# Attention and quantized feed-forward on one core: the up bias scaled as one row, and every queue in a new order

## What is computed

```
q = rope(RMS(LN(x)) * q_w)   k = rope(RMS(ctx) * k_w)   v = ctx        (16 query heads, 4 k/v heads of 32)
x = x + softmax(causal(q k^T / sqrt(32))) v  @ w_out^T
h = relu(LN(x) @ w_up + b_up + LN(x) @ A_up @ B_up)                    (2048 columns)
x = x + h @ w_down + b_down + h @ A_down @ B_down
```

## Time and profile before

| | |
|---|---|
| median of the runs | 482.93 us |
| profiled execution, its own time | 484.46 us |
| its span, first to last instruction | 482.7 us |
| mean granted TensorE clock | 0.979 |
| PE busy | 443.0 us (92%), 2416 matmuls |
| DVE busy | 352.0 us (73%) |
| ACT busy | 300.3 us (62%) |
| POOL (GpSimd) busy | 282.1 us (58%) |

### The profile page before, as it was taken

How to read it: one execution, slowest core, us unless ns; L and a number is a source line. 1 busy time by engine, 2 the same in 40 slices (tenths; PEclk the granted TensorE clock), 3 DMA queues, 4 the chain that set the end, 5 groups by cost and what they waited for, 6 DMA issues and landing times.

```text
span 482.7 us, 8285 instructions
## 1 busy us (share of the span) xinstructions
PE 443.0 (92%) x2416; PEld 218.2 (45%) x2416; DVE 352.0 (73%) x1076; ACT 300.3 (62%) x927; POOL 282.1 (58%) x304
## 2 busy tenths in 40 slices
PE   0285869999999999999999999999999999999997
PEld 0164545444444444444444444444444445444443
DVE  3899998979879786868686877778777856534341
ACT  1698978878858675757575757666675856422120
POOL 5477767685859574848384747576657745451100
PEclk9996879999999999999999999999999999999999
DMA  8679769789777858887867777897697777474422
GB/s 224 215 245 175 189 206 209 114 167 141 160 121 137 168 109 160 135 171 114 171 130 155 134 158 132 169 132 161 122 135 163 118 153 110 91 125 93 88 56 74
DMA packets 207740, 70.36 MB, mean 146 GB/s; under 512 B 196880, under 2 KB 200096, under 8 KB 207056
## 3 DMA queue, kind: packets, MB, share of 16 engines
q1 hardware_dynamic: 206864, 69.35, 72.7%
q10 hardware_dynamic: 752, 0.34, 0.3%
q0 software_dynamic: 80, 0.16, 0.2%
HBM read 17.15 MB, written 4.19 MB: 44 GB/s over the span
## 4 chain that ended last, share of the span: by engine, by line
PE 78%; DVE 1%; DMA 1%; SPq 0%; issue 0%
PE ff L951 33%; PE ff L937 33%; PE tb L919 8%; PE sb L891 2%; PE tb L907 2%; DMA x<-hid 1%; SPq L401 0%; PE tb L877 0%; DVE t_sin L1171 0%; DVE pr L1203 0%; DVE y L1253 0%; DVE stats L1184 0%; DVE x L1181 0%; DVE q L1212 0%; DVE q L1118 0%
## 5 line engine op out<-in xcount | busy, mean ns | idle before, releaser
L951 PE MATMUL ff<-wd_hi,x 128*128 128x512 f16 x512 | 152.3, 379 | 0.7 <-DMA x<-hid 0.7
L937 PE MATMUL ff<-wu_hi,xnT 128*128 128x512 f16 x512 | 152.7, 380 | 0.0
L691 ACT ACTIVATE pr<-pr,nmax 128x128 f32<-128x128 f32 x256 | 99.0, 389 | 13.6 <-DVE nmax L1203 12.9
L515 POOL TENSOR_TENSOR big<-pr,big 128x512 f16<-128x512 f32 x64 | 80.9, 1272 | 32.6 <-ACT big L722 32.6
L937 PE MATMUL ff<-wu_lo,xnT 128*128 128x512 f16 x256 | 97.0, 379 | 0.0
L951 PE MATMUL ff<-wd_lo,x 128*128 128x512 f16 x256 | 97.0, 379 | 0.0
L506 POOL TENSOR_TENSOR pr<-pr,rinv 128x512 f32<-128x512 f32 x64 | 72.7, 1137 | 35.6 <-DVE rinv L1111 35.6
L756 ACT ACTIVATE hid<-z 128x512 f16<-128x512 f32 x64 | 39.9, 624 | 80.1 <-DVE z L1132 80.1
L1203 DVE CUSTOM_DVE_ANT_0 pr<-sb,tabs,score_scale 128x128 f32<-128x128 f32 x256 | 73.8, 344 | 12.3 <-PE sb L891 11.2
L937 PEld LDWEIGHTS ff<-wu_hi,xnT 128*128 128x128 f16 x512 | 48.2, 98 | 58.4 <-issue 5.9
L1132 DVE SCALAR_TENSOR_TENSOR z<-ff,su,b_row 128x512 f32<-128x512 f32 x64 | 47.7, 745 | 36.0 <-PE ff L937 34.7
(11 more groups left out here) (144 smaller groups left out, 652.7 us busy)
## 6 DMA issues: line engine op xcount, KB each, us to landing
xt<-in_x SPq DMA_DIRECT2D x16, 256.0 KB, 3.0
big<-in_L_ffn_w_up_q SPq DMA_DIRECT2D x4, 1024.0 KB, 7.3
big<-in_L_ffn_w_down_q SPq DMA_DIRECT2D x4, 1024.0 KB, 6.2
out<-y SPq DMA_DIRECT2D x16, 256.0 KB, 2.7
wd_lo<-in_L_xattn_w_out SPq DMA_DIRECT2D x1, 1024.0 KB, 7.5
pT<-big SPq DMA_TRANSPOSE x64, 3.5
b_row<-in_L_ffn_b_up SPq DMA_DIRECT2D x1, 1024.0 KB, 9.1
x<-hid SPq DMA_TRANSPOSE x64, 3.2
```

The costliest lines, as they stand in the source:

```text
L515: pool.tensor_tensor(p3[:, m, :, 1, :], pr[:, m], p3[:, m, :, 0, :], ALU.subtract).then_inc(p_low, 1)
L691: last = act.activation(pr[:, m, g, :], pr[:, m, g, :], ACT.Exp, bias=nmax[:, p, j:j + 1], scale=-1.0, accum_out=rsum[:, p, j:j + 1])
L937: last = pe.matmul(bank[:], a[:, m, :], b[:, m, 512 * g:512 * g + 512], start=(m == 0 and i == 0), stop=(m == KC - 1 and i == 2))
L951: last = pe.matmul(ff[down_bank[n]][:], x2T[:, part, k + h % HG, :], b[:, h, :], start=(h == 0 and i == 0), stop=(h == HC - 1 and i == 2))
```

## The change

On the bias: DVE multiplies the 16x128 form of the row by the factor right after the factor is known (`b_scaled`, which lies in the tile z); SP stores these 8 KB to a row in memory (`bias_scaled_row`), and the load of `b_row` reads that row in place of b_up. ACT's four multiplications are gone. The store waits for DVE, the load for the store, and the load of weight group 2, which overwrites `b_flat`, now waits for DVE's multiplication too. z of batch 0 waits once, for the load.

On the order: nearly all slots change, PERIOD and FREE stay. The tiles that DVE dequantizes and those whose low part it makes are chosen anew (27 as before, and 26 for 25); the new slots were planned with longer transfer times. In SP's queue the first entries are now: load of w_out, batch 1, the three moves of LoRA rows, the LoRA factor, weight groups 1 and 2, transposes of q and k of batch 0, the bias store, weight group 3, the bias row. The diff, with the order's constants that the text speaks of:

```diff
@@ -24,84 +24,84 @@
-R_STATS = (0, 19, 407, 1366)
-R_MOMENTS = (2, 33, 483, 1400)
-R_SINES = (12, 110, 554, 1489)
-R_KLOW = (32, 211, 1015, 1496)
-R_QLOW = (18, 345, 975, 1516)
-R_QTURN = (409, 637, 1281, 1619)
-R_PTURN = ((687, 1308, 1751, 1921), (734, 1395, 1767, 2005), (1050, 1432, 1782, 2066), (1056, 1489, 1798, 2080))
-R_VLOW = (639, 1508, 2209, 2641)
-R_OLOW = (657, 1410, 1795, 2120)
-R_XNLOW = (934, 1660, 1960, 2268)
-R_XNTURN = (1268, 1739, 2015, 2244)
-R_UP = ((1254, 1861, 2175, 2525), (1381, 1898, 2244, 2538), (1526, 1935, 2251, 2553), (1632, 1993, 2290, 2592))
-R_Z = ((1159, 1746, 2046, 2325), (1202, 1776, 2109, 2385), (1302, 1864, 2172, 2440), (1467, 1896, 2216, 2495))
-R_X2LOW = ((1194, 1772, 2068, 2345), (1324, 1834, 2190, 2414), (1347, 1918, 2201, 2491), (1518, 1927, 2221, 2509))
-R_DOWN = ((1762, 2065, 2356, 2640), (1778, 2085, 2391, 2656), (1828, 2128, 2441, 2658), (1838, 2134, 2443, 2714))
-R_X2TURN = ((1555, 1867, 2159, 2401), (1563, 1894, 2179, 2428), (1599, 1914, 2205, 2467), (1620, 2002, 2216, 2468))
-DVE_TILES = (0, 1, 2, 3, 4, 5, 6, 7, 8, 9, 10, 12, 13, 14, 15, 16, 17, 18, 19, 20, 22, 23, 24, 25, 27, 28, 30)
-LOW_BY_DVE = (0, 1, 2, 5, 9, 10, 11, 14, 15, 16, 17, 18, 19, 20, 21, 22, 23, 24, 25, 26, 27, 28, 29, 30, 31)
-DEQ_AT = (17, 21, 22, 46, 60, 85, 87, 88, 99, 250, 281, 140, 288, 299, 466, 482, 560, 642, 653, 757, 837, 809, 941, 950, 1012,
-          1061, 1072, 1107, 1197, 1675, 1349, 1831)
-LOAD_AT = (379, 431, 567, 584, 1102, 1178, 1287)
-WO_LOAD_AT = 252
-ROW_LOAD_AT, DOWN_BIAS_LOAD_AT = 1243, 827
-BATCH_LOAD_AT = (116, 550, 1508)
-LORA_B_ROWS_AT = (381, 744)
-LORA_D_LOAD_AT, NORM_SCALES_AT = 115, 1
-BIAS_ROW_AT = (1091, 1190, 1384, 1460)
...
+R_STATS = (0, 52, 481, 1332)
+R_MOMENTS = (5, 179, 596, 1400)
+R_SINES = (35, 232, 818, 1547)
+R_KLOW = (68, 367, 1036, 1551)
+R_QLOW = (97, 484, 1125, 1593)
+R_QTURN = (230, 578, 1243, 1976)
+R_PTURN = ((734, 1503, 2000, 2418), (756, 1580, 2070, 2463), (972, 1597, 2150, 2472), (1062, 1673, 2167, 2491))
+R_VLOW = (981, 1711, 2708, 3025)
+R_OLOW = (1101, 1475, 1955, 2268)
+R_XNLOW = (1273, 1771, 2082, 2352)
+R_XNTURN = (1337, 2085, 2450, 2710)
+R_UP = ((1901, 2249, 2565, 2822), (1922, 2301, 2603, 2862), (2004, 2359, 2639, 2925), (2035, 2393, 2687, 2963))
+R_Z = ((1438, 1873, 2145, 2407), (1444, 1896, 2225, 2497), (1582, 2023, 2245, 2548), (1702, 2024, 2302, 2570))
+R_X2LOW = ((1548, 1929, 2219, 2480), (1581, 1943, 2269, 2537), (1681, 2028, 2301, 2561), (1716, 2056, 2317, 2574))
+R_DOWN = ((2131, 2439, 2712, 2973), (2140, 2447, 2724, 2988), (2212, 2463, 2751, 3037), (2216, 2490, 2792, 3065))
+R_X2TURN = ((1809, 2251, 2540, 2791), (1970, 2262, 2582, 2854), (1982, 2296, 2655, 2924), (2046, 2297, 2692, 2947))
+DVE_TILES = (0, 1, 2, 3, 4, 5, 6, 7, 8, 9, 11, 12, 13, 15, 16, 17, 18, 19, 21, 22, 24, 25, 27, 28, 29, 30, 31)
+LOW_BY_DVE = (2, 4, 6, 8, 9, 10, 11, 12, 14, 15, 16, 17, 18, 19, 20, 21, 22, 23, 24, 25, 26, 27, 28, 29, 30, 31)
+DEQ_AT = (7, 19, 20, 33, 109, 113, 165, 167, 204, 216, 281, 268, 339, 364, 349, 490, 568, 594, 619, 719, 909, 821, 984, 1036,
+          989, 1171, 1545, 1229, 1361, 1374, 1388, 1415)
+LOAD_AT = (174, 202, 334, 542, 726, 896, 1280)
+WO_LOAD_AT = 2
+ROW_LOAD_AT, DOWN_BIAS_LOAD_AT = 376, 1134
+BATCH_LOAD_AT = (97, 434, 1189)
+LORA_B_ROWS_AT = (115, 384)
+LORA_D_LOAD_AT, NORM_SCALES_AT = 125, 2
+BIAS_STORE_AT = 330
...
@@ -166,6 +166,9 @@
 
         s_up_flat, a_dn_flat = big[:, 4096:4096 + HC * C // QB], big[:, 4224:4224 + HC * R]
         b_flat = big[0:HC, 4480:4480 + P]
+
+        b_scaled = z[0:HC, 0, 0:P]
+        b_store = nc.dram_tensor("bias_scaled_row", (H,), F32).ap()
         R3 = 3 * R
 
         b_up_parts = high_area[:, 0:384].bitcast(F16).rearrange("p (k c) -> p k c", k=3)
@@ -247,7 +250,7 @@
         scale_steps, scales_ready = sem("scale_steps"), sem("scales_ready")
         tables_ready, pool_consts = sem("tables_ready"), sem("pool_consts")
         norm_scale_steps = sem("norm_scale_steps")
-        bias_row_in, bias_scaled = sem("bias_row_in"), sem("bias_scaled")
+        bias_row_in, bias_scaled, bias_stored = sem("bias_row_in"), sem("bias_scaled"), sem("bias_stored")
         a_high, a_low, b_high, b_low = sem("a_high"), sem("a_low"), sem("b_high"), sem("b_low")
         ident_cast, minus_cast = sem("ident_cast"), sem("minus_cast")
         a_turned, a_copied = sem("a_turned"), sem("a_copied")
@@ -360,6 +363,7 @@
                     sp.wait_ge(w_turned, 4 * (g - W_RING + 1))
                 if g == 2:
                     sp.wait_ge(tops_ready, 7)
+                    sp.wait_ge(bias_scaled, 1)
                 src = wuq_v[g] if g < 4 else wdq_v[g - 4]
                 sp.dma_start(stage_i[:, g % W_RING], src).then_inc(wq_in[g % W_RING], 16)
 
@@ -433,8 +437,12 @@
                     sp.dma_start(a_nat[:, KC * R:].rearrange("p (g a) -> p g a", a=4 * R), wda_v).then_inc(a_dn_in, 16)
                 if s == WO_LOAD_AT:
                     sp.dma_start(wo_raw, wo.rearrange("(j p) c -> p j c", p=P)).then_inc(wout_in, 16)
+                if s == BIAS_STORE_AT:
+                    sp.wait_ge(bias_scaled, 1)
+                    sp.dma_start(b_store.rearrange("(p a) -> p a", p=HC), b_scaled).then_inc(bias_stored, 16)
                 if s == ROW_LOAD_AT:
-                    sp.dma_start(b_row[:], bu.rearrange("(a n) -> a n", a=1).broadcast_to([P, H])).then_inc(bias_row_in, 16)
+                    sp.wait_ge(bias_stored, 16)
+                    sp.dma_start(b_row[:], b_store.rearrange("(a n) -> a n", a=1).broadcast_to([P, H])).then_inc(bias_row_in, 16)
                 if s == DOWN_BIAS_LOAD_AT:
                     sp.dma_start(bd_bc[:], bd.rearrange("(a n) -> a n", a=1).broadcast_to([P, C])).then_inc(down_bias_in, 16)
                 n = at(s, R_STORE)
@@ -606,12 +614,6 @@
                     act.wait_ge(wout_in, 16)
                 act.activation(wo_nat[:, j, :].rearrange("p (n g d) -> p n g d", g=NG, d=HD),
                                wo_raw[:, j, :].rearrange("p (g n d) -> p n g d", g=NG, d=HD), ACT.Copy).then_inc(wo_ordered, 1)
-
-            def bias_row(g):
-                act.wait_ge(scale_steps, SCALE_STEPS)
-                act.wait_ge(bias_row_in, 16)
-                part = b_row[:, 512 * g:512 * g + 512]
-                act.activation(part, part, ACT.Identity, scale=kap[:, 5:6]).then_inc(bias_scaled, 1)
 
             def lora_a_high(down):
                 if down:
@@ -781,8 +783,6 @@
                         weights_low(t)
                 attention(s)
                 for m in range(4):
-                    if BIAS_ROW_AT[m] == s:
-                        bias_row(m)
                     if WO_ORDER_AT[m] == s:
                         wout_order(m)
                     if WO_HIGH_AT[m] == s:
@@ -1055,6 +1055,7 @@
                 dve.tensor_scalar(s_up[:, 0:4, :], s_up[:, 0:4, :], kap[:, 0:1], None, ALU.mult).then_inc(scales_ready, 1)
                 dve.tensor_scalar(s_dn[:], s_dn[:], kap[:, 1:2], None, ALU.mult).then_inc(scales_ready, 1)
                 link(dve.tensor_scalar(kap[:, 5:6], kap[:, 4:5], X2_TOP, None, ALU.mult))
+                dve.tensor_scalar(b_scaled, b_flat, kap[0:HC, 5:6], None, ALU.mult).then_inc(bias_scaled, 1)
                 link(dve.tensor_scalar(su[:], power[:, 0:1], kap[:, 5:6], -1.0 / XN_SCALE, ALU.mult, ALU.mult), wait=False)
                 link(dve.tensor_scalar(sd[:], power[:, 1:2], power[:, 4:5], 1.0 / X2_TOP, ALU.mult, ALU.mult), wait=False)
                 assert step[0] == SCALE_STEPS
@@ -1127,8 +1128,8 @@
                         dve.wait_ge(up_done, 4 * n + g + 1)
                         if 4 * n + g >= 2:
                             dve.wait_ge(x2_low, 4 * n + g - 1)
-                        if n == 0:
-                            dve.wait_ge(bias_scaled, g + 1)
+                        if n == 0 and g == 0:
+                            dve.wait_ge(bias_row_in, 16)
                         dve.scalar_tensor_tensor(z[:, g % 2], ff[up_bank[n, g]][:], su[:], b_row[:, 512 * g:512 * g + 512],
                                                  ALU.mult, ALU.add).then_inc(ff_read, 1)
```

94 lines of the change are left out of this document (47 added, 47 removed).

## The result

The changed kernel took **490.66 us** in the median of 4 runs (490.0 to 492.19), the kernel before 483.08 beside it (482.84 to 484.92): ratio **1.0146**, 95% interval 1.0125 to 1.0167, so slower by about 7 us. The forecast was 483.9, its range 480.3 to 488.5: the sign was right, the size was not. The profiled execution of after took 490.0 us with a span of 488.2, 5.5 more than the 482.7 of before. It is the fastest of its four, and that of before (484.46) lies 1.5 above its median, so the two profiles differ by 5.5 us where the medians differ by 7.6: some 2 us of the loss stand in neither profile.

What follows compares the result with a forecast made beforehand. The start was taken as bound by DVE's queue, PE gapless after it. DVE's +2.6, first loads' +0.3 and SP's -1.95 gave +0.95 us on 482.93: 483.9 us, range 480.3 to 488.5.

Steps and rivals of the forecast that it cites:

- The bias costs nothing: Bias path: ACT's 2.8 us less gains nothing, DVE's product costs 0.2 us, SP's store and load 0.
- DVE's queue ahead of hidden_low 0.3, +2.6 and +0.3: Start: extra DVE work including the bias adds 2.6 us; the first 25 us, with moved weight loads, add 0.3.
- rival (b): Start: the moved load of tiles 4 to 7 lands late and delays DVE's queue; +4 us, 486.9, chance 0.15.
- SP gives 1.95 back: Handover: hidden_low 0.3 no longer meets a busy SP, so its transpose issues at once; -1.95 us.
- PE can keep up with this: Start: PE's work before DOWN0.3 is the same within 0.2 us, only in other order.
- first up product near 79: Start: six more tiles turned first move PE's first up product from 72.66 to near 79 us.
- The lower clock: Start: sign of being wrong, the first up product held by PE's clock at 1.2 GHz, the lower level.
- The period at 0: Steady period of 264 slots: the new order costs nothing, 0 us.
- The slacks that were checked (xnT, v's low part): Period: xnT's transpose keeps 1.0 us of slack, v's low part on POOL some 2 us.
- Rival (c): Period: POOL's v low part or heads_out's misses pv or proj by half a microsecond, some 12 periods; +6, 489, chance 0.08.
- Rival (a), fewer collisions: Start: DVE and POOL collide less, a third less of 8.6 us lost; -2.9, so 480.9 us, chance 0.23.

Runs made afterwards that it cites:

- the run on before: Kernel before, with the transpose of batch 0's last hidden part issued on SP ahead of batch 3's queries: 485.20 us, ratio 1.0039.
- vsum's place: Changed kernel with pT.3 ahead of kT, queries' transpose ahead of two loads, vsum moved just ahead of the first scores: 489.32 us, ratio 1.0105.
- pT.3 first: Changed kernel, with the transpose of the probabilities' last part issued on SP ahead of the keys' transpose in the period: 488.32 us, ratio 1.0086.
- before, pT.3 late: Kernel before, with the transpose of the probabilities' last part issued on SP behind the keys' transpose in the period: 485.64 us, ratio 1.0033.

## Why the prediction was wrong, point by point

- **The bias costs nothing: right.** 1.0010 by itself in the old order, 0 to 0.8 us in the new. DVE's product took 0.29 us where 0.2 was put down. ACT's 2.8 us brought no gain, as costed.
- **DVE's queue ahead of hidden_low 0.3, +2.6 and +0.3: 0.6 short.** It began at 101.66 us against 98.14, +3.5 instead of +2.9. In the first 25 us the weight loads were issued at 19.79 (forecast about 19) and tile 4 was taken up at 25.82 (forecast 24.2). Its load landed at 25.4, so it too came later than forecast, but DVE was not there yet and did not wait for it, so rival (b) did not happen: DVE waited 1.28 us for ACT's part of q, a row that the prediction did not look for.
- **SP gives 1.95 back: wrong by 0.8.** pT2.0 stands in the place of qT3 as said and issues at 101.77, so the hidden part's transpose left 0.78 us after its data instead of 1.95: 1.2 gained. Nor was the step worth its length: the run on before shows that alone it gives nothing. These 0.8 and the 0.6 above are 1.4 us: by this chain alone DOWN0.3 could start at about 106.4, not at 104.95.
- **"PE can keep up with this", first up product near 79: the step that failed at the start.** It was at 81.39. From there to DOWN0.3 PE has 24.7 us of work and 0.6 of idle time (106.67 - 81.39 = 25.3), so 79 would have been just enough for 104.95, and in after PE is what ends last, 0.3 us behind the chain above. Work that PE must do was counted, but not the time at which it could start: the chain of batch 0's norm was not followed in the new order (its transpose landed only at 79.9), nor the two loads ahead of qT2 (3.19 us of PE's time). The lower clock, which the prediction named as a sign of being wrong, has a share: two groups of transposes at 76.32 and 77.60 took 1.06 us instead of 0.60. How the 2.4 us divide among these is open, since taking single ones away moved nothing.
- **The period at 0: the second step that failed, and the larger**, worth 2.9 us in the profile. The slacks that were checked (xnT, v's low part) did hold. The one that gave way was not on the list: kT moved ahead of pT.3 on SP, where it waits for PE, and pT.3 waits behind it. Rival (c) had the picture (the same short gap of PE before pv again and again, behind the slack of half a microsecond) and the wrong cause, at 0.08. Gaps of 0.56 to 0.65 us came in 3 of the periods of the profile instead of all 12: 1.8 us, not 6. The period itself is 0.05 us longer as well, and that no step of the prediction foresaw.
- **Rival (a), fewer collisions: wrong.** Dequantizations took 809 ns (14 of them) and 955 (13) in the mean against 843 and 1002, and 0.8 us less in all (23.1 of DVE's busy time against 23.9); the first up product came later all the same.

The loss of about 7 us is thus some 2.9 (give or take 1.4) for pT.3, 0.5 for vsum's place, and some 2.7 for a late start. For the start two pairs of profiles agree: pv of batch 2 is 2.63 us later in after than in before, and 2.77 later in "pT.3 first" (117.23) than in "before, pT.3 late" (114.46), whose starts are those of after and before. About 1 us is left that no profile shows. No version was found that beats the kernel before. The best of the new order that leaves nothing out, 1.0086, is still slower.
